# Projections of a two-layer model: x comes in from the host with its channels on the partitions too, and the means and roots of its rows are spread over the partitions through DRAM

## Reference

```python
xn = _layernorm(x, axis=-1)            # (x - mean) / sqrt(var + 1e-5) over 512 channels
x1 = xn @ w1_w.T + w1_b                # then depthwise conv of 3 tokens, silu -> z
v = _silu(xn @ v1_w.T + v1_b)
...
x_ssm = _ssm(x_conv, A, B_ssm, C_ssm, D_ssm)
out = x_ssm * v @ w2_w.T + w2_b        # plus a quantised linear layer of xn
...
```

## Time and profile before

| | before |
|---|---|
| median of 3 runs | 2112.29 us (2111.44 to 2112.76) |
| the profiled execution | 2113.2 us, its span 2111.4 us |
| instructions | 27601 |
| end of the last projection product, start of the scan | 395.0 us into the span |
| share of the span, PE / DVE / ACT / POOL | 99 / 70 / 52 / 40% |
| DMA | 241.40 MB, 114 GB/s in the mean |
| granted TensorE clock | 0.998 of full speed |

### The profile page before, as it was taken

The page is one execution under the profiler, slowest core; times in us unless marked ns, Lnnn a source line. Parts: engine busy times, 40 slices in busy tenths (PEclk is TensorE's granted clock), DMA queues, the critical chain, the costliest instruction groups (busy, mean ns, idle before and its releaser), DMA issues.

```text
span 2111.4 us, 27601 instructions
## 1 busy us (share of the span) xinstructions
PE 2082.4 (99%) x9467; PEld 1669.0 (79%) x9467; DVE 1476.9 (70%) x2884; ACT 1092.2 (52%) x1834; POOL 840.7 (40%) x844
## 2 busy tenths in 40 slices
PE   7999999999999999999999999999999999999998
PEld 6888888644578888888888888778888888888887
DVE  4776555576687777776777875567677767676776
ACT  4554555423355555555555554755544555555443
POOL 1021000254544545454455454144444444444454
PEclk9999999999999999999999999999999999999999
DMA  4333533677543333333333333422222222222211
GB/s 153 120 130 129 170 121 107 231 250 234 180 130 106 114 112 118 102 119 100 120 127 104 106 114 102 170 78 71 70 70 70 70 90 90 86 84 70 70 41 41
DMA packets 174838, 241.40 MB, mean 114 GB/s; under 512 B 19049, under 2 KB 109417, under 8 KB 173930
## 3 DMA queue, kind: packets, MB, share of 16 engines
q1 hardware_dynamic: 161576, 216.10, 31.2%
q10 hardware_dynamic: 13122, 23.53, 3.0%
HBM read 138.86 MB, written 100.73 MB: 113 GB/s over the span
## 4 chain that ended last, share of the span: by engine, by line
PE 93%; DVE 3%; ACT 1%; issue 1%; POOL 1%; DMA 1%; SPq 0%; POOLq 0%; ACTq 0%; DVEq 0%
PE bank L102 23%; PE bank L104 23%; PE bank L103 23%; PE bank L1383 8%; PE bank L1939 3%; PE bank L778 3%; PE bank L799 3%; PE bank L796 3%; PE bank L1339 2%; PE bank L496 1%; PE bank L1397 0%; DMA d_v<-scr_v 0%; DVE e_w_lo L1765 0%; DVE d_x L1235 0%; DVE d_magic L1209 0%
## 5 line engine op out<-in xcount | busy, mean ns | idle before, releaser
L102 PE MATMUL bank<-e_ring,e_w_hi 128*128 128x512 f32 x512 | 200.8, 392 | 0.0
L103 PE MATMUL bank<-e_ring,e_w_hi 128*128 128x512 f32 x512 | 199.3, 389 | 0.0
L104 PE MATMUL bank<-e_ring,e_w_lo 128*128 128x512 f32 x512 | 199.3, 389 | 0.0
L1383 PE MATMUL bank<-d_kh,d_nat 128*128 128x512 f32 x768 | 192.7, 400 | 0.0
L1659 POOL TENSOR_TENSOR e_x<-e_x,e_beta 128x512 f32<-128x512 f32 x64 | 91.6, 1450 | 222.0 <-ACT e_y L1702 221.9
L1004 POOL TENSOR_TENSOR rstd<-d_var_eps,neg_half 128x1 f32<-128x1 f32 x64 | 35.7, 558 | 348.0 <-DVE d_var_eps L1246 348.0
L1713 ACT ACTIVATE e_kr<-bank 128x512 f32<-128x512 f32 x64 | 38.0, 594 | 248.4 <-PE bank L104 248.4
L1383 PEld LDWEIGHTS bank<-d_kh,d_nat 128*128 128x128 f32 x768 | 140.8, 190 | 27.3
L1783 DVE TENSOR_TENSOR e_ring<-e_mixed,e_ring 128x512 fp32r<-128x512 f32 x128 | 93.2, 729 | 89.7 <-ACT e_ring L1677 89.6
L1641 POOL TENSOR_TENSOR e_x<-e_x,e_ff 128x512 f32<-128x512 f32 x64 | 83.4, 1303 | 177.0 <-DVE e_ff L1850 177.0
L1251 DVE TENSOR_TENSOR d_nat<-d_xn,d_nat 128x512 fp32r<-128x512 f32 x64 | 85.9, 1344 | 77.7 <-ACT d_nat L1111 77.7
(11 more groups left out here) (210 smaller groups left out, 6296.1 us busy)
## 6 DMA issues: line engine op xcount, KB each, us to landing
scr_v<-b_vt SPq DMA_DIRECT2D x64, 256.0 KB, 2.6
scr_z<-b_zt SPq DMA_DIRECT2D x64, 256.0 KB, 2.1
c_z<-scr_z SPq DMA_DIRECT2D x64, 256.0 KB, 4.1
scr_y<-c_y ACTq DMA_DIRECT2D x64, 256.0 KB, 3.8
d_x<-in_L_attn_x SPq DMA_DIRECT2D x64, 256.0 KB, 4.1
scr_x<-d_x SPq DMA_DIRECT2D x64, 256.0 KB, 2.5
scr_xnt<-d_xt SPq DMA_DIRECT2D x32, 512.0 KB, 4.1
e_xt<-scr_xnt SPq DMA_DIRECT2D x16, 1024.0 KB, 5.7
```

What stands on the lines that cost most here:

```text
L102: eng.matmul(out, lhs[hi], rhs[hi], start=first, stop=False, skip_group_check=onto)
L103: eng.matmul(out, lhs[hi], rhs[lo], start=False, stop=False, skip_group_check=onto)
L104: return eng.matmul(out, lhs[lo], rhs[hi], start=False, stop=last, skip_group_check=onto)
L1383: mm = pe.matmul(BG[c][:, :], s[:, i, cols], r[:, j, :], start=M % NTB == 0 and i == j, stop=M % NTB == NTB - 1 and i == 1, skip_group_che ...
```

## The change

The host lays x out a second time, `x_turned`, with channels on the partitions. Group 0 goes as before: normalised with tokens on the partitions and turned by PE, now into four banks (`turn_first`). For groups 1 to 15 PE turns nothing. Tokens still come in (`xg`, now one buffer) for the statistics alone. Means and roots of a group, two columns of 128x4, are stored to DRAM (`store_rows`) and read back as rows to all partitions (`load_rows`, 512 KB written). The 1 MB of channels come into the one buffer `xc` (`load_channels`) once the low parts of the group ahead are made. POOL subtracts the row of means (`less_mean`), DVE multiplies by the row of roots (`times_root`); the rows are read with a step of four elements (16 bytes). High and low parts are made from `xc`, two pairs between the side taps instead of after them all. The statistics are a group further ahead. Semaphores of other stages are shared, which changes counts only.

```diff
-    xg = [sb(f"b_xg{h}", [P, GT, D]) for h in range(2)]
+    xg = sb("b_xg", [P, GT, D])
+    xc = sb("b_xc", [P, KT, GN])
+    rows = sb("b_rows", [P, 2, GN])
-    TB, XB, VB, KB = banks[0:2], banks[2:4], banks[4:6], banks[6:8]
+    XB, VB, KB = banks[2:4], banks[4:6], banks[6:8]
+    TB = banks[0:2] + banks[6:8]
+    def channels(kt):
+        return xc[:, kt, :].rearrange("p (a i) -> p a i", a=GT)
+    def row(w):
+        return rows[:, w, :].rearrange("p (i a) -> p a i", a=GT)
...
+        def load_channels(g):
+            if g == 1:
+                sp.wait_ge(t_full, KT)
+            else:
+                sp.wait_ge(lo_done, KT * g)
+            sp.dma_start(xc[:, :, :], ins["x_turned"][g]).then_inc(xc_in, 16)
+        def store_rows(g):
+            sp.wait_ge(stat, 4 * g + 4)
+            for w, name in enumerate(("mean0", "rstd0")):
+                sp.dma_start(scr["rows"][g, w], keep[name][:, g * GT:(g + 1) * GT])\
+                  .then_inc(rows_out, 16)
+        def load_rows(g):
+            sp.wait_ge(rows_out, 32 * g)
+            if g > 1:
+                sp.wait_ge(xn_done, KT * g)
+            sp.dma_start(rows[:, :, :].rearrange("p w t -> p (w t)"),
+                         scr["rows"][g].rearrange("w i a -> (w i a)").rearrange("(o t) -> o t", o=1)
+                         .broadcast_to([P, 2 * GN])).then_inc(rows_in, 16)
...
         for g in range(NG):
+            if g + 3 < NG:
+                sp.wait_ge(stat, 4 * (g + 2) + 1)
+                load_x(g + 3)
             if g + 2 < NG:
-                sp.wait_ge(t_full, KT * (g + 1))
-                load_x(g + 2)
+                store_rows(g + 2)
+                load_channels(g + 2)
+                load_rows(g + 2)
...
+        def less_mean(g):
+            pool.wait_ge(xc_in, 16 * g)
+            pool.wait_ge(rows_in, 16 * g)
+            for kt in range(KT):
+                nc.gpsimd.tensor_tensor(channels(kt), channels(kt), row(0), ALU.subtract).then_inc(less_done, 1)
...
         for g in range(NG):
-            rstd_of(g)
...
+            if g + 1 < NG:
+                less_mean(g + 1)
+            if g + 2 < NG:
+                rstd_of(g + 2)
+            if g in (3, 4, 5, 6):
+                power_bit(g - 3)
...
+        def times_root(g):
+            for kt in range(KT):
+                dve.wait_ge(less_done, KT * g + kt + 1)
+                nc.vector.tensor_tensor(channels(kt), channels(kt), row(1), ALU.mult).then_inc(xn_done, 1)
...
         def body(g):
             if g + 1 < NG:
-                normalise(g + 1)
+                times_root(g + 1)
+            if g + 2 < NG:
+                statistics(g + 2)
             for kt in range(KT):
                 for c in units_in(g):
                     side_terms(c, kt)
-            if g + 1 < NG:
-                for kt in range(KT):
-                    low_part(g + 1, kt)
+                if g + 1 < NG and kt < 2:
+                    low_part(g + 1, 2 * kt)
+                    low_part(g + 1, 2 * kt + 1)
...
+                if g + 1 < NG and m in (1, 2):
+                    high_part(g + 1, 2 * m - 2)
+                    high_part(g + 1, 2 * m - 1)
...
-                if g + 1 < NG and m in (0, 2):
-                    turn_x(g + 1, m)
-                    turn_x(g + 1, m + 1)
+    laid["x_turned"] = raw["L0_attn_x"].reshape(2, 256, 8, 2, KT, P).transpose(0, 2, 5, 4, 3, 1).reshape(16, P, KT, 512)
```

More of the change, by code:

```diff
@@ L134, in phase_project @@
     kpad = sb("b_kpad", [OCTET, NO, 2 * CHUNK])
-    const_in, tab_in = sem("b_const_in"), sem("b_tab_in")
-    x_in = [sem(f"b_x_in{h}") for h in range(2)]
+    rows = sb("b_rows", [P, 2, GN])
+    const_in, tab_in = sem("b_const_in"), keep["tables_in"]
+    x_in, xc_in = sem("b_x_in"), sem("b_xc_in")
+    rows_out, rows_in = sem("b_rows_out"), sem("b_rows_in")
     x_head = keep["x_ld"]
     w_in = [sem(f"b_w_in{i}") for i in range(2)]
-    w_hi, w_lo, w1_lo = keep["w_hi"], keep["w_lo"], sem("b_w1_lo")
+    w_hi, w_lo, less_done = keep["w_hi"], keep["w_lo"], sem("b_less_done")
     stat = sem("b_stat")
@@ L167, in phase_project, with x_stat, normalised @@
     }
+    def x_stat(g):
+        return xg if g else xc
+    def channels(kt):
+        return xc[:, kt, :].rearrange("p (a i) -> p a i", a=GT)
+    def row(w):
+        return rows[:, w, :].rearrange("p (i a) -> p a i", a=GT)
+    def normalised(g, kt):
+        return xc[:, kt, :] if g else TB[kt][:, :]
     def x1_row(b, r, kt):
@@ L400, in body @@
                 state_powers(range(3) if g == 3 else (3,))
-        normalise(0)
+        statistics(0)
+        normalise_first()
         for kt in range(KT):
             low_part(0, kt)
+        statistics(1)
         for g in range(NG):
@@ L409, in high_part @@
         def high_part(g, kt):
-            act.wait_ge(t_full, KT * g + kt + 1)
-            nc.scalar.activation(xt[g % 2][:, 0, kt, :], TB[kt % 2][:, :], ACT.Copy).then_inc(hi_done, 1)
+            if g:
+                act.wait_ge(xn_done, KT * g + kt + 1)
+            else:
+                act.wait_ge(t_full, kt + 1)
+            nc.scalar.activation(xt[g % 2][:, 0, kt, :], normalised(g, kt), ACT.Copy).then_inc(hi_done, 1)
         def weight_high(i, tile, raw):
@@ L850, in phase_mix @@
     ones = rest("d_ones", [P, 1])
-    const_in, sums_set, bias_done = sem("d_const_in"), sem("d_sums_set"), sem("d_bias_done")
+    const_in, sums_set, bias_done = keep["rows_in"], sem("d_sums_set"), sem("d_bias_done")
     x_ld = keep["x_ld"]
@@ L1545, in phase_second_layer @@
     shift1 = keep["shift1"]
-    const_in = sem("e_const_in")
+    const_in = keep["rows_in"]
     w_in = [sem(f"e_w_in{i}") for i in range(4)]
@@ L2034, in two_layer_kernel @@
         "out": out,
+        "rows": dram("scr_rows", [sh.NG, 2, P, sh.GT]),
         "kern": dram("scr_kern", [NO, OCTET, 2 * CHUNK]),
```

89 lines of the change are left out of this document (43 added, 46 removed).

## The result

| | before | after |
|---|---|---|
| median | 2112.46 us (2111.44 to 2112.76) | 2178.28 us (2176.76 to 2178.72) |
| the profiled execution | 2113.2 us, span 2111.4 | 2178.1 us, span 2176.3 |
| first product of the scan | 395.0 us | 461.9 us |
| granted clock | 0.998 | 0.984 |

The ratio is 1.0312 (95% interval 1.0299 to 1.0324). The forecast was 2150 in a range of 2108 to 2190: slower as forecast, and by more. All of the loss lies in the projections: the scan starts 66.9 us later, the execution ends 64.9 us later.

What follows compares the result with a forecast made beforehand. PE was taken to bound the kernel, busy 99%. Removing 27.5 us of turning made a 25.3 us round the limit; fourteen rounds, start and powers put the scan at 432.0 against 395.0, +37 us: 2150, range 2108 to 2190.

Steps and rivals of the forecast that it cites:

- last low part to POOL's start: Head of each round: channels and rows load and land, POOL wakes; 6.6 us, bounds 5.6 and 10.6.
- subtract and multiply: Middle of each round: four POOL subtractions with DVE products behind them, blocking and stride included; 8.9 us, bounds 6.2 and 10.4.
- The loop: Projections: load, subtract and multiply, statistics, side taps and low parts form a round of 25.3 us, against PE's 21.75.
- The signs named: Projection trace: period some 25 us, PE, POOL and DVE waits, products over 1 us, scan near 432, three periods near 29.
- The load: SP's queue: 1 MB of channels lands in 5.2 us, rows add 1.3; stores of z and v cost nothing.
- The clock: PE after its waits: products at the lower level take twice as long, 3.5 us to spare, costed at nothing.
- POOL is the slow one: Rival, POOL's strided subtraction takes 1.67 to 1.76 us: 2172 to 2178; chance 0.24, shared with late landings.
- Powers: POOL's power_bit beside side taps and low parts: DVE held up 4.2 us three times plus 0.8, 13.4 us.
- The sum: Projections: first low parts end at 46.7, fourteen rounds of 25.3, less 4.4, plus 13.4: 409.9; scan at 432.0.
- The round stays short: Rival, no blocking between POOL and DVE, free stride: round 22.6, 2096, or 2092 with short landings; faster, chance 0.13.
- blocking without stride cost: Rival, subtract and multiply takes 7.3 us, 1.6 less in 15 rounds: 2126; chance 0.15 for 2117 to 2137.
- No change: Rival, short landings with blocking give a round of 23 to 23.5; within 0.2% of before, chance 0.06.

Runs made afterwards that it cites:

- e1: The changed kernel with SP issuing the load of the rows ahead of the load of the channels: 2174.84 us, ratio 1.0299.
- e7: e1 with SP's stores of z and v held back until the channels have landed: 2151.58 us, ratio 1.0186.
- e3: The changed kernel, POOL and DVE reading the rows element after element, so means and roots meet wrong tokens: 2139.28 us, ratio 1.0127.
- e2: The changed kernel with two channel buffers, their load issued first, and kpad passing through the place of toep_t in halves: 2123.15 us, ratio 1.0051.
- e4: The changed kernel with the subtraction of the mean moved from POOL to DVE, which then does both row operations: 2151.52 us, ratio 1.0187.
- e5: The changed kernel with nine POOL power instructions (j = 1 to 3) on 64 of 1024 columns: 2165.43 us, ratio 1.0254.
- e11: The changed kernel with the edits of e7 and e4, POOL copying the rows into a packed tile, kpad stored in halves: 2102.95 us, ratio 0.9954.
- e12: e11 with the ten POOL power instructions spread one per group over groups 3 to 12, where DVE waits: 2094.49 us, ratio 0.9920.
- e9: The changed kernel with two channel buffers, both row operations on DVE, and rows packed by a store of 4-byte elements: 2134.20 us, ratio 1.0105.

## Why the forecast was right in kind and short in size

| term of the round | forecast | measured | |
|---|---|---|---|
| last low part to POOL's start | 6.6 | 7.9 | stores behind the loads: e1, e7 |
| subtract and multiply | 8.9 | 9.7 | POOL's step: e3 |
| statistics | 4.4 | 4.3 | |
| side taps and low parts | 5.4 | 5.3 | |
| round | 25.3 | 27.2 | |

**The loop** was right: one buffer ties load, POOL, DVE, statistics and low parts into a ring. The signs named are there: PE's gaps put down to ACT, POOL idle for `b_rows`, DVE for POOL (87.7 us), products of 2.08 us in the mean. Two are there only in part: the three periods are 31.5 to 31.8, not near 29, and the scan's first product comes at 461.9, not near 432. e2 takes one link out and gets 55 us back, e7, e3 and e4 shorten links and get 27, 39 and 27.

**The load** failed at one step: the stores of z and v behind it were costed at nothing, since ACT needs them two groups later and the DMA share was low. Right for who waits for the stores, wrong for what they do to the load ahead of them. The rows landed after 7.1 us, not some 6.1. With the rows issued ahead and the stores held back, 5.9 us are left where the sum had 6.6; no run holds the stores back with the rows still behind the channels, so how the term divides between the two stays open. The expectation of e1 made the same mistake once more. The stores themselves are slower too: those of v land after 6.1 us and those of z after 7.1, before after 2.6 and 2.1. The clock, which the forecast put at nothing as well, did cost nothing inside the rounds (no link of PE in the chain), but did behind the last one (below).

**Subtract and multiply.** Blocking was forecast and is there: a product of 1.06 us alone (forecast 1.05) takes 2.40 beside a subtraction (the median). The Trainium skill's rule of the port pair taken in turns (SBUF — State Buffer, "SBUF: two separate sides") agrees: 9.7 us in turns, 7.9 on DVE alone. The term was short by POOL's subtraction, costed at the packed price of 1.30 though it reads with the same step for which the product was charged: it is 1.53. Four times 0.23 (1.53 for 1.30) is 0.9, about the 0.8 by which the term is short. This is the rival "POOL is the slow one" at half its price (1.67 to 1.76); that its total of 2172 to 2178 meets the result is chance, as most of the excess comes from the load. The Trainium skill's half as much again for such steps (GPSIMD Engine Reference, "Performance pitfalls for Q7 kernels") is not what is seen here, with one of two operands read so: 1.53 against 1.28 is a fifth. For DVE, where a step of 16 bytes made 1.06 out of 0.68, the Trainium skill's rule that an access to another 16-byte line each time costs more (Advanced Engine Details and Errata, "Memory Cachelines") agrees.

**Powers**: 13.4 forecast; the three periods are 31.8, 31.8 and 31.5 instead of 27.1, and the one before them 27.9: some 14.5. The cover was gone as argued; e5 shows 12.9 for nine of the ten instructions.

**The sum.** The channels of group 2 are issued at 45.4 (forecast 46.7). The fourteen rounds with the powers take 389.7 us to the last low part at 435.1, where the sum has 363.2: +26.5. Then one step more failed: PE's last group was to start 0.3 us behind that. PE's timeline around it, the stretch behind its last stop (busy by engine, clock 0.60), and the first product of the scan:

```profile
432.96 0.50 PE L102 MATMUL bank<-b_xt,b_v 128*128 128x512 f32 x1 [3.05 <-ACT b_vt L535]
...
440.13 0.39 PE L102 MATMUL bank<-b_xt,b_w 128*128 128x512 f32 x1
```

```profile
432.96:436.00 3.04, 3.04 (x8) 2.46 (x9) 2.97 (x6) 1.67 (x3) 0.74 (x1) 0.60 0.39 140
```

```profile
461.92 2.21 PE L846 MATMUL bank<-c_z,c_into 128*128 128x512 f32 x4
```

The forecast let ACT's silu and one bank of products (2.7) end about at the last low part. But PE still had two `v` banks of group 14 to do, 24 products, and they took 7.2 us instead of 5.4, as those from 433.9 to 436.9 came 0.43 us apart instead of 0.23, at the lower level of the clock. So it started at 440.1, 5.0 behind: 2.7 for the second bank and 1.8 for the clock, besides the 0.3 of the forecast. Inside the rounds this costs nothing, since PE waits again anyway; at the end it does. This is read from the trace, no run tested it. -1.3 + 26.5 + 4.7 = 29.9, the difference between 461.9 and 432.0. Some 2 us are given back by the end of the execution.

**The other rivals.** "The round stays short" and "blocking without stride cost" fell with e3 and e4: both costs are there. "No change" needed short landings.

## What to carry over

When a change makes a transfer wait for a buffer's last reader and that reader for the transfer, write the ring out with each link's time and compare it with the bounding engine's work: below it the ring is free (e11, e12, with the same single buffer), above it every microsecond counts once per group. Cost what is issued behind a load on the same queue as part of that load, and charge the step of an operand to every engine that reads it. Work split over DVE and POOL on SBUF tiles can take longer than on DVE alone; POOL is best given what fits where DVE waits.

## What the runs showed of the hardware

- A load of 1 MB with eight stores of 256 KB issued right behind it lands after 7.0 us (e1), with the stores held back after 5.9 (e7); 512 KB of rows after 7.1 between that load and the stores (the changed kernel), and 3.9 ahead of the load (e1).
- Storing 128x4 values in elements of 4 bytes takes 8.8 us to landing (e9), in pieces of 16 bytes 3.0 (the changed kernel).
- Reading one of two operands with a step of 16 bytes: 1.06 us instead of 0.68 on DVE (128x512), 1.53 instead of 1.28 on POOL (the changed kernel and e3). A copy by POOL of the same step took 1.06 us while DVE did nothing (two in 2.13, e11).
